# Evacuating a head's four y blocks from PSUM with one ScalarE copy into one strided SBUF buffer

## What is computed

```python
def gla_recurrence(q, k, v, g):              # per batch and head, K = V = 128, H = 16
    def step(S, inp):
        qt, kt, vt, gt = inp
        S = S * exp(gt)[..., None] + kt[..., None] * vt[..., None, :]
        return S, einsum('bhk,bhkv->bhv', qt, S)
    ...

def attn(x):
    q = (x @ Wq.T) * K ** -0.5;  k = x @ Wk.T;  v = x @ Wv.T
    g = log_sigmoid(x @ Wg.T)
    y = gla_recurrence(q, k, v, g)
    return layernorm(y, gamma, beta) @ Wo.T

def ffn(x, weight):
    w_q = clip(round(weight / mean(abs(weight))), -1, 1)
    beta = max(abs(x), axis=-1) / 127
    return (clip(round(x / beta), -127, 127) @ w_q.T) * mean(abs(weight)) * beta

x = x + 0.5 * ffn(ln(x), w)
x = x + attn(ln(x))
x = x + 0.5 * ffn(ln(x), w)
```

## Time and profile before

| | |
|---|---|
| time, median of 3 runs | 8933.89 us (8772.52 to 9072.19) |
| the profiled execution, its own time | 8709.51 us |
| its span (slowest core, core 4) | 8708.0 us |
| spans of the eight cores | 8660.7 to 8708.0 us |
| TensorE matmul busy | 4423.1 us, 51% |
| VectorE busy | 4295.4 us, 49% |
| ScalarE busy | 2461.2 us, 28% |
| mean granted TensorE clock, core 4 | 0.766 of full speed |

### The profile page before, as it was taken

The page is one execution under the profiler, slowest core; times in us unless marked ns, Lnnn a source line. Parts: engine busy times, 40 slices in busy tenths (PEclk is TensorE's granted clock), DMA queues, the critical chain, the costliest instruction groups (busy, mean ns, idle before and its releaser), DMA issues.

```text
span 8708.0 us, 90362 instructions; the slowest of 8 cores (8660.7 to 8708.0 us)
## 1 busy us (share of the span) xinstructions
PE 4423.1 (51%) x30210; PEld 2888.4 (33%) x30210; DVE 4295.4 (49%) x5028; ACT 2461.2 (28%) x3840; POOL 220.6 (3%) x408
## 2 busy tenths in 40 slices
PE   0003742667245762568334772458525673457753
PEld 0002421453134421454223531344214531345332
DVE  5512157523756248442667138461575237562456
ACT  0211233223223232323323232222332232232312
POOL 1000000000000000000000000000000000000000
PEclk9999875879568885789657885688758895688866
DMA  6497310243012410233012520133102430123212
GB/s 203 132 297 199 113 43 0 78 121 102 0 39 79 125 59 0 68 102 109 22 29 53 140 80 0 52 94 112 44 0 78 121 100 2 39 73 114 65 39 58
DMA packets 956776, 693.81 MB, mean 80 GB/s; under 512 B 118656, under 2 KB 929664, under 8 KB 941984
## 3 DMA queue, kind: packets, MB, share of 16 engines
q1 hardware_dynamic: 923136, 520.15, 21.5%
q0 software_dynamic: 33184, 167.88, 6.5%
HBM read 620.84 MB, written 83.89 MB: 81 GB/s over the span
## 4 chain that ended last, share of the span: by engine, by line
DVE 39%; PE 35%; DMA 10%; ACT 7%; issue 6%; DVEq 1%; ACTq 0%; SPq 0%; POOL 0%; POOLq 0%
PE pj L218 33%; DVE uw L209 14%; DVE S L209 8%; DVE st L209 4%; ACT xqT L213 3%; DMA fat<-s_f 2%; ACT y L213 2%; DVE mtile L209 2%; DVE mnx L209 2%; DVE qs L209 2%; DVE bq L209 2%; DVE y L209 1%; PE pT L338 1%; DMA qs<-fw 1%; DMA fat<-s_o 1%
## 5 line engine op out<-in xcount | busy, mean ns | idle before, releaser
L218 PE MATMUL pj<-fat,xqT 128*128 128x256 bf16 x12288 | 1452.3, 281 | 470.7 <-DVE x1b L209 168.3
L218 PE MATMUL pj<-xl2T,hw 128*128 128x512 bf16 x6144 | 1511.0, 411 | 325.1 <-ACT sg L213 257.4
L218 PEld LDWEIGHTS pj<-fat,xqT 128*128 128x128 bf16 x12288 | 1218.7, 100 | 704.1 <-issue 532.1
L209 DVE SCALAR_TENSOR_TENSOR uw<-bq,uw 128x1024 f16<-128x1024 f16 (+1 forms) x704 | 1067.4, 1516 | 78.1 <-DVE uw L209 1.4
L218 PEld LDWEIGHTS pj<-xl2T,hw 128*128 128x128 bf16 x6144 | 632.7, 104 | 1165.8 <-issue 564.7
L209 DVE TENSOR_TENSOR sg<-sg,gb 128x512 f32<-128x512 f32 x128 | 88.6, 692 | 1444.6 <-ACT gb L213 1444.6
L213 ACT ACTIVATE bq<-uw,bias 128x1024 f16<-128x1024 f16 x512 | 587.6, 1148 | 282.7 <-DVE uw L209 282.3
L218 PE MATMUL pj<-v,fat 32*128 32x128 bf16 x2048 | 302.7, 299 | 554.8 <-DVE S L209 554.8
L218 PE MATMUL pj<-S,xqT 128*32 128x128 bf16 x512 | 107.4, 287 | 853.2 <-DVE S L209 604.8
L338 PE MATMUL pT<-identt,hw 128*128 128x128 bf16 x512 | 70.7, 291 | 915.4 <-DVE S L209 679.5
L218 PE MATMUL pj<-fat,xl2T 128*128 128x256 bf16 x4096 | 468.5, 279 | 55.8 <-DMA fat<-s_v 55.1
(11 more groups left out here) (134 smaller groups left out, 4905.0 us busy)
## 6 DMA issues: line engine op xcount, KB each, us to landing
hw<-s_qkg SPq DMA_DIRECT2D x256, 768.0 KB, 6.6
fat<-s_f SPq DMA_DIRECT2D x256, 512.0 KB, 5.4
fat<-s_v SPq DMA_DIRECT2D x128, 512.0 KB, 5.4
fat<-s_o SPq DMA_DIRECT2D x128, 512.0 KB, 5.4
out<-ost POOLq DMA_DIRECT2D x256, 128.0 KB, 3.3
s_qkg<-y SPq DMA_DIRECT2D x48, 512.0 KB, 10.1
ost<-fw POOLq DMA_DIRECT2D x16, 1024.0 KB, 5.9
qs<-fw POOLq DMA_DIRECT2D x16, 1024.0 KB, 6.3
```

Source lines behind the costliest of these rows:

```text
L209: return p.emit("vector", lambda e, a=args, k=kw: getattr(e, meth)(*a, **k), inc="VD")
L218: e.matmul(o, l, r, start=s0, stop=s1, tile_position=t, skip_group_check=sk),
```

## The change

The four buffers `ysl[t]` become column ranges of one buffer `ysl_all` of 128 x 8192, bf16 (the same bytes in all). In the head loop the four copies of 128 x 128 become one copy of 128 x 4 x 128, whose destination runs over the four row tiles with a step of 2048 elements; it reads the whole of the bank `pY`. The other edits write the same ranges of the same buffer in another way.

```diff
-        ysl = [sb(f"y_{t}", [128, D], BF16) for t in range(TPS)]
+        ysl_all = sb("y_all", [128, TPS * D], BF16)
+        ysl = [ysl_all[:, t * D:(t + 1) * D] for t in range(TPS)]
...
                 p.wait("scalar", "TD", td_y)
-                for t in range(TPS):
-                    yevac_sd = s_op("copy", ysl[t][:, h * HK:(h + 1) * HK],
-                                    pY[:, 128 * t:128 * (t + 1)])
+                ydst = ysl_all[:].rearrange("p (t d) -> p t d", d=D)[:, :, h * HK:(h + 1) * HK]
+                yevac_sd = s_op("copy", ydst,
+                                pY[:, 0:512].rearrange("p (t c) -> p t c", c=128))
...
                 for gg in range(4):
+                    ysl_slice = ysl_all[:, t * D + gg * 512: t * D + (gg + 1) * 512]
                     vd_evac[gg] = v_op("scalar_tensor_tensor",
-                                       ysl[t][:, gg * 512:(gg + 1) * 512],
-                                       YB[gg][:], 1.0,
-                                       ysl[t][:, gg * 512:(gg + 1) * 512],
-                                       ALU.mult, ALU.add)
-                tile_stats(t, ysl[t], dump=nt)
+                                       ysl_slice, YB[gg][:], 1.0,
+                                       ysl_slice, ALU.mult, ALU.add)
+                tile_stats(t, ysl_all[:, t * D:(t + 1) * D], dump=nt)
...
-                vd = v_op("tensor_scalar", nt[:], ysl[t][:], mu[:, t:t + 1],
-                          rstd[:, t:t + 1], ALU.subtract, ALU.mult)
+                vd = v_op("tensor_scalar", nt[:], ysl_all[:, t * D:(t + 1) * D],
+                          mu[:, t:t + 1], rstd[:, t:t + 1], ALU.subtract, ALU.mult)
```

## The result

The changed kernel takes 8642.51 us (median of 10 runs, 8494.0 to 8958.55), the kernel before in the same comparison 8925.28 us (median of 10 runs). The ratio of the two is 0.9755 with a 95% interval of 0.965 to 0.986: 2.45% less, which is clear of no change but not of 2%. The profiled execution took 8508.83 us where that of before took 8709.51.

The account below looks back on a forecast made before the run. No engine was near full; a chain changing engines set the time. 94 us direct plus 90 us clock made 184 us: 8525 us in the profiled execution, 8745 us off the median, range 8510 to 8880 us.

Parts of the forecast that it names:

- 585 ns, upper end 1060: ScalarE's merged y copy from pY: 585 ns expected, 1060 ns if each of four ranges cost like its own copy.
- The rival with a costlier copy: Strided y copy costs like four; only three hand-overs a head go, 33 us gained, 8676 us; chance 0.03.
- the rule that the prediction took from the Trainium skill: ScalarE copies: about 0.3 us per activation plus 0.83 ns per element; gain 0.90 us a head, 115 us in sum.
- Direct gain: ScalarE's y copies between pY and sg: 1.40 to 0.67 us, 0.73 us for each of 128 heads, 94 us.
- The clock: TensorE in the head loops: shorter waits give back 90 of 164 us lost at half clock; chance 0.50 for 55 to 120.
- a straight line in the sum of TensorE's two waits: Clock loss between projections: none at 1.89 us, 164 us at 3.40; at 2.67 us 85 stay lost, 79 come back.
- If the longest single wait decides: TensorE's wait for sg, 1.55 us, is below the 1.89 that kept the clock; all 164 us come back.
- If the waits add up: TensorE's two waits between projections sum to 2.67 us, above the 2.42 that lost the clock; drops go on.
- the clock gives nothing back: Rival for the head loops: each gap keeps its clock drop, only 94 us come, 8615 us; chance 0.17.
- all of it comes back: Rival for the head loops: all gaps keep full clock, 258 us gained, 8451 us; chance 0.22.
- The longer drop as the rule: Rival for the head loops: nearly all heads show the long drop, 16.62 us each, 8741 us; chance 0.08.

Follow-up runs that it names:

- the run with the copy moved away: Changed kernel with the one y copy of each head moved into the next head's gate work, behind the log; span 8287.5 us.
- two copies: Changed kernel with two y copies of two row tiles each in place of the one; second run 8553.0 to 8587.3 us over the cores.
- before, 4 fillers: Kernel before plus four unneeded 512-column matmuls behind those into pY; cores 0 to 3 took 8625.2 to 8657.1 us, cores 4 to 7 8685.6 to 8732.4.
- changed, 4 fillers: Changed kernel plus four unneeded 512-column matmuls behind those into pY; slowest core 8486.6 us.
- before, fillers in both: Kernel before plus unneeded matmuls in both TensorE waits, two behind pA and six behind pY; slowest core 8555.1 us.
- the layout alone: Changed kernel with the four y copies put back, one buffer kept; span 8779.8 us, then cores 0 to 3 8697.8 to 8722.9, other die up to 8785.6.
- the four copies moved: Kernel before, its four y copies and four buffers kept, copies moved into the next head's gate work; cores 4 to 7 took 8275.9 to 8308.1 us.

## Why the prediction was right

**The copy.** "585 ns, upper end 1060" came out at 586 ns, and 0.67 us with the hand-over. The row that decided, the copy to xl2T with its four ranges, was the right one to go by. The rival with a costlier copy doesn't hold. By the rule that the prediction took from the Trainium skill ("ScalarE: Activation LUTs", section "Rules for kernel authors") a head would have gained 0.90 us, 0.17 more than the trace shows; that rule is for an activation with its bias as a pointer operand, which these copies don't have.

**Direct gain.** 0.73 us for each of 128 heads, 94 us: heads at full clock went from 14.76 to 14.03 us, the wait for sg from 2.28 to 1.55, both as forecast. Nothing else in the loops became late; the run with the copy moved away shows that the chain over VectorE has room for a head of 12.7 us too.

**The clock.** Taken at 90 us; it was 109 on the profiled cores and 98 as a mean of eight. The order of the sum was right and the size a little low. The step that gave it was a straight line in the sum of TensorE's two waits, with no loss at 1.89 us. The runs give its true course, as means over the eight cores (in the fourth line over cores 0 to 3, scaled from the seven loops of each that are not at 0.81):

| kernel | the two waits, us | sum | heads with a drop | lost to the clock, us |
|---|---|---|---|---|
| before | 1.12 + 2.28 | 3.40 | 70% | 155 |
| two copies | 1.12 + 1.79 | 2.91 | 35% | 82 |
| changed | 1.12 + 1.55 | 2.67 | 22% | 57 |
| before, 4 fillers | 1.12 + 1.43 | 2.55 | 23% | 57 |
| changed, 4 fillers | 1.12 + 0.69 | 1.81 | 11% | 33 |
| before, fillers in both | 0.69 + 1.00 | 1.69 | none | 14 |

The waits of the second, the fourth and the fifth line:

```profile
2979.93 10.52 PE L219 MATMUL pj<-xl2T,hw 128*128 128x512 bf16 x48 [1.79 <-ACT sg L214]
...
6032.36 10.52 PE L218 MATMUL pj<-xl2T,hw 128*128 128x512 bf16 x48 [1.43 <-ACT sg L213]
...
2934.28 7.93 PE L219 MATMUL pj<-xl2T,hw 128*128 128x512 bf16 x36 [0.69 <-ACT sg L214]
```

The line would have left 111 us for two copies and 85 for the change, and nothing at 1.81 us. It was too high in the middle and had its foot in the wrong place: drops go on below the 1.89 us of the feed-forward phase, and about 14 us never come back, since they belong to the start of the loop. The two errors partly cancelled, so that the 90 us came so near is in part luck.

The line's lower end rested on two single waits, 1.89 us with the clock kept and 2.42 us with it lost. The same phase shows that such a wait decides nothing by its length alone. Some 25 us earlier TensorE waited 2.67 us, longer than either, and went on at 1.00:

```profile
3655.29 1.91 PE L218 MATMUL pj<-fat,xqT 128*128 128x256 bf16 x16 [2.67 <-DVE x1b L209]
...
3655.30:3657.20 1.90, 1.90 (x16) 1.46 (x16) 1.80 (x2) 1.12 (x2) 0.00 (x0) 1.00 1.17 324
```

Over all cores of before, of the waits in feed-forward phases that began at full clock, none of the 528 of 1.9 us shows a lower clock up to 1.8 us behind its end, and 92 of the 138 of 2.4 us do. What a shorter wait changes is how often a drop comes, and the prediction should have reckoned in such shares.

**The bounds of the clock's part.** "If the longest single wait decides" is refuted: the changed kernel's longest is 1.55 us in nearly all heads, with fillers 1.12 us, both below the 1.89 that kept the clock in another phase, and both still lose time. "If the waits add up" is nearer, but it isn't a matter of one value either; the share of heads with a drop fades with the sum. That the sum alone decides isn't shown: the last two lines of the table are 0.12 us apart in it, and their shares 11% and none.

**The rivals.** That the clock gives nothing back is refuted by the 98 us. That all of it comes back is out as well: with fillers in both waits 14 us stayed, at the loop's start, and the change alone left 57. The longer drop as the rule did not come: of the 62 heads that had it before none is left, and the loss fell in every run that shortened the waits.

**The time.** For the profiled execution 8525 us were worked out and 8508.8 measured. The share off the median, 2.1%, was 2.45% in the comparison. The stated 8745 us lies 1.2% above the median of 8642.5, because the median of the new kernel's runs stood nearer to its profiled execution (1.6% above) than that of the three runs of before to theirs (2.6%). The prediction carried the distance of those three runs over to the new kernel; why it is smaller there isn't shown.

## What to carry to other kernels

Price a short operation by the wait it stands in: 0.7 us of ScalarE between two bursts of matmuls cost 0.73 us directly and about as much again in TensorE's clock (94 and 98 us in all). Before merging operations in such a place, look whether they have to stand there; moved into a wait of ScalarE they cost nothing, merged or not, and the head was 1.3 us shorter still. Where a wait can't be shortened, matmuls that nobody needs can fill it: they took 153 us off the kernel before and 21 off the changed one.

## What I had not expected of the hardware

A granted clock between the two levels, held for long: in both runs of the layout alone, in the first run with two copies, in that with four fillers on the kernel before and in that with the four copies moved, TensorE's busy stretches stood at 0.81, on one die or on both. Core 0 of the run with four fillers, inside one loop:

```profile
7950.00:8000.00 50.00, 42.56 (x183) 18.46 (x186) 15.51 (x27) 18.45 (x40) 0.00 (x0) 0.81 0.32 95
8000.00:8050.00 50.00, 42.28 (x184) 18.37 (x186) 13.30 (x24) 18.46 (x39) 0.00 (x0) 0.81 0.32 95
...
8026.00:8027.00 1.00, 0.32 (x5) 0.34 (x6) 0.43 (x1) 0.03 (x1) 0.00 (x0) 0.81 0.44 69
8027.00:8028.00 1.00, 1.00 (x6) 0.26 (x3) 0.00 (x0) 0.57 (x3) 0.00 (x0) 0.81 0.95 316
```

Single microseconds show 0.81 too, one with TensorE mostly idle and one with it busy throughout. So here a value between 0.50 and 1.00 isn't a mixture of the two, as it is in the profile of before; a head's projection takes 12.8 us there where it takes 10.5 at full clock. That loop took 264.6 us where the core's other seven took 231 to 236. The level came for part of a run, in kernels of before's speed as well as in faster ones. What sets it off was not tried. Two of my expectations, of the first run of the layout alone and of the four fillers on the kernel before, were missed mainly by it, so the clock of every core has to be read before a span is compared.
